# Local attention scored per 32 queries against their 160 keys, with merged scratch round trips

## What is computed

```python
h = shift_token(x)
q, k, v = split(h @ wqkv)              # 8 heads of 64
q, k = rotary_xpos(l2norm(q) * qs, l2norm(k) * ksc)
# windows of 128 queries; keys of the window before and of the own one
mask = (i < j) | (i > j + 128) | (j == -1)
attn = softmax(where(mask, -max, 8 * q @ k.T))
x = x + (attn @ v) @ wo
h = layernorm(shift_token(x)) * lg + lb
a, g = split(h @ w1 + b1)
x = x + (a * gelu(g)) @ w2 + b2
```

## Time and profile before

| | |
|---|---|
| median of 3 runs | 4971.94 us (4968.18 to 4976.64) |
| the profiled execution's own time | 4966.22 us |
| its span | 4964.4 us |
| granted clock, mean over the span | 0.959 |
| PE, DVE, ACT, POOL busy | 91%, 72%, 60%, 49% |

### The profile page before, as it was taken

The page is one execution under the profiler, slowest core; times in us unless marked ns, Lnnn a source line. Parts: engine busy times, 40 slices in busy tenths (PEclk is TensorE's granted clock), DMA queues, the critical chain, the costliest instruction groups (busy, mean ns, idle before and its releaser), DMA issues. The chain is left out here.

```text
span 4964.4 us, 269505 instructions
## 1 busy us (share of the span) xinstructions
PE 4507.8 (91%) x107928; PEld 3817.4 (77%) x107928; DVE 3564.7 (72%) x10345; ACT 2979.7 (60%) x8486; POOL 2441.6 (49%) x3196
## 2 busy tenths in 40 slices
PE   7898898678888888666999999999999999999998
PEld 6888888678888888654777777777777777777777
DVE  4666666568878887475777777777777777777775
ACT  5777777534444444354666666666666666666665
POOL 1222222267777777203555555555555555555554
PEclk8999999789999999788999999999999999999999
DMA  2343343467777777694555666555565555555554
GB/s 87 87 96 93 93 98 89 114 143 165 165 165 163 167 164 161 175 299 126 170 170 168 173 174 171 172 171 171 180 196 175 173 173 172 171 171 173 173 175 131
DMA packets 1283528, 775.96 MB, mean 156 GB/s; under 512 B 686800, under 2 KB 1179088, under 8 KB 1282256
## 3 DMA queue, kind: packets, MB, share of 16 engines
q1 hardware_dynamic: 1231888, 700.43, 53.1%
q10 hardware_dynamic: 51392, 73.02, 5.0%
HBM read 410.44 MB, written 362.68 MB: 156 GB/s over the span
## 5 line engine op out<-in xcount | busy, mean ns | idle before, releaser
L2367 ACT ACTIVATE l_prob<-l_prob,l_nb,l_rq 128x256 f32<-128x256 f32 x1024 | 601.6, 590 | 20.8 <-DVE l_nb L2193 13.1
L2033 POOL TENSOR_TENSOR l_prob<-l_prob,l_rinv 128x512 f32<-128x512 f32 x512 | 526.8, 1039 | 108.4 <-DVE l_rinv L2173 108.4
L2017 POOL TENSOR_TENSOR l_k<-l_kn,l_tab 128x512 f32<-128x512 f32 x128 | 162.5, 1270 | 614.8 <-DVE l_kn L2165 614.8
L2559 PE MATMUL lD<-l_hid,w 128*128 128x128 f32 x3072 | 364.0, 275 | 0.0
L2559 PEld LDWEIGHTS lD<-l_hid,w 128*128 128x128 f32 x3072 | 353.3, 192 | 0.0
L2551 PEld LDWEIGHTS lA<-l_hn,w 128*128 128x128 f32 x2048 | 242.9, 195 | 110.1 <-POOL l_hn L2051 61.1
L2202 DVE STREAM_TRANSPOSE l_pb<-l_prob 128x512 f32<-128x512 f32 x512 | 326.6, 676 | 0.6 <-POOL l_prob L2033 0.5
L2027 POOL TENSOR_TENSOR l_qr<-l_q 128x512 f32<-128x512 f32 x128 | 162.4, 1269 | 328.1 <-DVE l_q L2131 328.1
L1097 POOL TENSOR_TENSOR sc_aqx<-sc_late,sc_headmask 128x256 f32<-128x256 f32 x256 | 170.8, 667 | 278.9 <-PE sc_Y L1190 277.2
L1173 PE MATMUL sc_AB<-sc_aq,sc_bkx 32*32 32x32 f32 x16384 | 257.3, 198 | 37.4 <-POOL sc_bkx L1097 29.1
L497 POOL TENSOR_TENSOR rk<-rk,bkraw 128x256 f32<-128x256 f32 x64 | 54.6, 871 | 477.9 <-DVE bkraw L383 477.9
(11 more groups left out here) (276 smaller groups left out, 13707.3 us busy)
## 6 DMA issues: line engine op xcount, KB each, us to landing
scratch_pz<-l_pb SPq DMA_DIRECT2D x256, 512.0 KB, 3.0
l_pT<-scratch_pz SPq DMA_DIRECT2D x1024, 128.0 KB, 3.2
scratch_cm<-cm SPq DMA_DIRECT2D x64, 512.0 KB, 4.1
scratch_qz<-l_q SPq DMA_DIRECT2D x128, 256.0 KB, 2.9
l_qT<-scratch_qz SPq DMA_DIRECT2D x512, 64.0 KB, 2.0
scratch_kz<-l_k SPq DMA_DIRECT2D x128, 256.0 KB, 2.8
l_kT<-scratch_kz SPq DMA_DIRECT2D x512, 64.0 KB, 2.9
sc_early<-scratch_cm ACTq DMA_DIRECT2D x59, 512.0 KB, 4.7
```

Of the source, the lines that this page charges most:

```text
L2017: tt(k1[s][:], kn[s][:], wide(2, slice(0, DH)), ALU.mult)
L2033: tt(prob[s][:, pair], prob[s][:, pair], rinv[s][:, pair].unsqueeze(2).broadcast_to([P, 2, 2 * P]), ALU.mult).then_inc(Q["pn"][s].sem, 1)
L2367: last_ = nc.scalar.activation(prob[s][:, h], prob[s][:, h], ACT.Exp, scale=rq8[s][:, h:h + 1], bias=nb[s][:, h:h + 1], accum_out=sums[s][ ...
L2559: last_ = mm(bank[s][3][:, c * P:(c + 1) * P], w2[:, m, c * P:(c + 1) * P], hid[s][:, m], start=(c == 0 and m == 0), stop=(c == CC - 1 and ...
```

## The change

- **Scores.** A head pair's two matmuls (128 weight columns, 256 moving columns) become eight: for each of the four blocks of 32 queries and each head one matmul with 64 rows and 32 columns of weights, and the 160 keys that those queries can reach as moving columns.
- **Width.** `prob` is 160 wide instead of 256. Mask, maximum, exponential, normalisation and transposes work on 160 columns. The mask is one constant table `wm` with a second plane for a sequence's first window; the per-stream masks, their setup and `remask` are gone.
- **q and k.** Both are turned into one tile `qk`, written by one DMA (512 KB) and read by four (128 KB each) into the ring `qkT` of three places; in halves with w == 0 of the unit read, four more DMAs (64 KB each) put k in a second place. The write waits for both `q_turned` and `k_turned`. Before, q was read at the start of the half; now the reads stand between P's write and P's reads.
- **P.** One write of all eight heads (640 KB instead of twice 512 KB) behind the fourth `turn_p`, and eight reads of 32 to 128 KB, which all stand behind the reads of q and k. `values` waits once, at pair 0, for all eight.
- Some waits of TensorE become instructions of their own (`free_pe`), and `pT` is cleared once at the start.

```diff
                 def write_qk(s, u):
                     sp.wait_ge(S["q_turned"][s].sem, S["q_turned"][s].after(u))
+                    sp.wait_ge(S["k_turned"][s].sem, S["k_turned"][s].after(u))
...
+                    sp.dma_start(a["qkz"][s], qk[s][:].rearrange("p j y h t -> p (j y h t)")).then_inc(S["qk_out"][s].sem, 16)
+
+                def read_qk(s, u, w):
...
+                    turned = a["qkz"][s].rearrange("(i c) (j n) -> j c i n", i=BL, j=BL)
+                    cur = (2, 1)[w] * BL
                     for j in range(BL):
+                        sp.dma_start(qkT[s][32 * j:32 * j + 32, cur:cur + BL].rearrange("p i y h t -> p i (y h t)"),
+                                     turned[j]).then_inc(S["qkT"][s].sem, 16)
+                    if w == 0:
+                        for j in range(BL):
+                            sp.dma_start(qkT[s][32 * j:32 * j + 32, 0:BL, 1].rearrange("p i h t -> p i (h t)"),
+                                         turned[j][:, :, 32 * NHP:]).then_inc(S["kT"][s].sem, 16)
...
+                def write_p(s, u):
+                    sp.wait_ge(Q["p_turned"][s].sem, Q["p_turned"][s].after(u * NHP + NHP - 1))
...
+                def read_p(s, u):
...
                     for j in range(BL):
+                        for slot, lo, hi in ((0, 0, j + 1), (1, j, BL)):
+                            start = s * P * row + lo * 32 * row + (j + BL * slot - lo) * n
+                            sp.dma_start(pT[s][32 * j:32 * j + 32, lo:hi, slot].rearrange("p i h t -> p i (h t)"),
+                                         bass.AP(a["pz"].tensor, start, [[row, 32], [32 * row - n, hi - lo], [1, n]])
+                                         ).then_inc(H["pT"][s].sem, 16)
...
-                    write_p(s, u, 0)
                     if within(un):
-                        write_k(o, un)
-                    write_p(s, u, 1)
-                    read_p(s, u, 0)
+                        write_qk(o, un)
+                    write_p(s, u)
                     if within(un):
-                        read_k(o, un, wn)
-                    read_p(s, u, 1)
+                        read_qk(o, un, wn)
+                    read_p(s, u)
...
-                    for x in range(2):
-                        rows_ = slice(x * DH, (x + 1) * DH)
-                        last_ = mm(scored(s, hp, x), qT[s][rows_, :, hp], kT[s][rows_, :, :, hp].rearrange("p x i t -> p (x i) t"),
-                                   start=True, stop=True)
+                    own, back = (2, 1)[w] * BL, (1, 0)[w] * BL
+                    for i in range(BL):
+                        for x in range(2):
+                            rows_ = slice(x * DH, (x + 1) * DH)
+                            last_ = mm(scored(s, hp, x)[32 * i:32 * i + 32], qkT[s][rows_, own + i, 0, hp],
+                                       qkT[s][rows_, back + i:back + i + NR, 1, hp], start=True, stop=True)
...
-                    if hp % 2 == 0:
-                        pe.wait_ge(H[g]["pT"][s].sem, H[g]["pT"][s].after(u))
                     if hp == 0:
+                        pe.wait_ge(H["pT"][s].sem, H["pT"][s].after(u))
```

More of the change, by code:

```diff
@@ L1761, in local_stage @@
         rot, tab = two("rot", [P, 4, DH]), two("tab", [P, 4, DH])
-        wm = one("wm", [P, 2 * P])
+        wm = one("wm", [P, 2, SPAN])
         mean_w, pause, least = one("mean_w", [P, P]), one("pause", [P, NB]), one("least", [P, 1])
         x1s, dsqs = two("x1s", [P, P]), two("dsqs", [P, P])
-        mask = [two(f"mask{s}_", [P, 2, P]) for s in range(NB)]
         hT = [two(f"h{s}_", [P, CC, P + 1]) for s in range(NB)]
@@ L1789, in local_stage @@
         O = signals(nc, ctx, "oT", 2, "lg", ahead=4)
-        H = [signals(nc, ctx, "p_out:16 pT:64", 2, f"lg{g}_") for g in range(2)]
+        H = signals(nc, ctx, "p_out:16 pT:128", 2, "lh")
         I = [signals(nc, ctx, "h_in:8 rot_in:8", 2, f"li{w}_") for w in range(2)]
-        start_signals(nc, tuple(sems.values()), R, S, Z, Q, M, O, *H, *I)
+        start_signals(nc, tuple(sems.values()), R, S, Z, Q, M, O, H, *I)
         tab_made = R["tab"][0]
@@ L2259, in first @@
                     dve.wait_ge(sems["set"], 1)
-                    for s in range(NB):
-                        nc.vector.tensor_copy(mask[s][0][:, 0, :], wm[:, P:2 * P])
-                        last = nc.vector.tensor_copy(mask[s][1][:].rearrange("p x n -> p (x n)"), wm[:])
-                    last.then_inc(sems["prep"], 1)
-                    dve.wait_ge(sems["prep"], 1)
                     for s in range(NB):
@@ L2587, in half @@
                     if mlp:
-                        values(o, um, 0, layer(um, l))
-                        values(o, um, 1, layer(um, l))
+                        values(o, um, wm_, 0, layer(um, l))
+                        values(o, um, wm_, 1, layer(um, l))
                     scores(s, u, w, 0)
@@ L2594, in half @@
                     if mlp:
-                        values(o, um, 2, layer(um, l))
-                        values(o, um, 3, layer(um, l))
+                        values(o, um, wm_, 2, layer(um, l))
+                        values(o, um, wm_, 3, layer(um, l))
                     scores(s, u, w, 2)
@@ L2707, in lay_out @@
     out["eye16"] = np.ascontiguousarray(np.broadcast_to(np.eye(CH, dtype=np.float32), (P, 2, CH, CH)))
-    q, kx = np.arange(P)[:, None], np.arange(P)[None, :]
-    neg = np.float32(MASKED)
-    before, own = np.where(kx < q, neg, 0), np.where(kx > q, neg, 0)
-    out["winmask"] = np.concatenate([before, own], axis=1).astype(np.float32)
+    row, r = np.arange(P)[:, None], np.arange(160)[None, :]
+    neg, behind = np.float32(MASKED), r - row % 32
+    near = np.where((behind < 0) | (behind > P), neg, 0)
+    begin = np.where(r < P - row // 32 * 32, neg, near)
+    out["winmask"] = np.stack([near, begin], axis=1).astype(np.float32)
     n = out["x"].shape[1]
```

127 lines of the change are left out of this document (49 added, 78 removed).

## The result

The changed kernel takes 5199.26 us (median of 4 runs, 5196.34 to 5200.36) against 4970.42 before (4 runs): a ratio of 1.0457, 95% interval 1.0439 to 1.0476. It is 229 us slower.

A forecast was written before the change was run, and what follows sets the result against it. The prediction took PE's own list as the bound, with the chain through P's round trip close behind. It summed 4966 + 157 (wait) + 25 (clock) = 5148, as a median 5154 us, 3.7% slower; 8 in 10 range 4990 to 5380.

The forecast's parts named there:

- the forecast case's own range: Total time if the forecast case holds: 5060 to 5220 us, chance 0.59.
- The wait: PE at pair 0's values waits for P's last read in nearly every half, 1.3 and 3.2 us in turns.
- the predicted 7.94: Start of the mean's matmul behind the values' start, 0.9 us earlier than the 8.84 of before.
- 15.4: Issue of P's first read, us behind the values' start, in halves with four reads of q and k.
- the 2.8 taken: Seven steps from P's first read to its eighth in the issuing queue: 2.8 us, between 2.0 and 3.3.
- the wait term: Halves lengthened from 20.66 to 21.9 us by the wait for P's last read: 157 us over 127 halves.
- I allow 0.2 us per half, 25 us: Allowance for stretches at 1.2 GHz at a half's start that lengthen the chain.
- rival 2: The clock falls: 3 of 7.9 us of PE chain work at 1.2 GHz, 5250 to 5350 us; chance 0.17.
- its sign: What would show the falling clock: a granted clock under 1.00 in the steady part.
- the bounds it names: Behind the range 5060 to 5220: pace 2.1 to 3.3, landing 2.5 to 3.2, called 0.6 us either way.
- Rival 3: Narrow score tiles do not run side by side: 1.1 us more per block than before, 5550 us; chance 0.04.
- Rival 1: Quick reads, seven P steps in 2.1 and landing 2.5, leave PE the bound: about 4905 us; chance 0.15.

The follow-up runs named there:

- e1: Changed kernel with the four reads of k's second copy moved behind P's eight reads in SyncE's list; 5043.27 us, ratio 1.0144.
- e5: Changed kernel with k turned and q and k written early; SyncE's order then P's write, four q/k reads, P's reads, k's second copy; 4919.11 us.
- e6: e5 with P's second and fourth normalisations earlier on GpSimd and its first transposes ahead of the mean's subtraction on VectorE; 4838.66 us, ratio 0.9743.
- e2: Changed kernel with k turned early and the write and reads of q and k ahead of P's write in SyncE's list; 5179.01 us, ratio 1.0418.
- e8: Changed kernel with P again in two pieces of four heads, each with one write and eight reads, in the order of before; 5410.64 us, ratio 1.0891.
- e3: Changed kernel with the values' matmuls taking the identity and not waiting for P's reads, all transfers kept; wrong output; 4816.12 us, ratio 0.9685.
- e7: Changed kernel with 1 or 3 idle matmuls of 512 columns ahead of the wait for P, in both layers; 5187.38 us, ratio 1.0443.
- e9: Changed kernel with 1 or 3 idle matmuls of 512 columns ahead of the wait for P in layer 0 alone; 5169.58 us, ratio 1.0404.
- e4: Changed kernel with 4 or 12 idle matmuls of 128 columns on the identity ahead of the wait for P; 5270.50 us, ratio 1.0607.
- e10: Changed kernel with five idle matmuls of 8 columns per half of layer 0, ahead of the wait for P; 5205.08 us, ratio 1.0475.

## Why the prediction was right, and which term was off

The forecast, 5154, was 45 us under the result, which lies in the forecast case's own range.

**The wait.** Right in place and cause. PE waits for `l_pT<-scratch_pz` at the values of pair 0 in every half, 257 us in 2500. That SyncE's list is the reason is shown from both sides: e1, e5 and e6 move issues and turns of SyncE, VectorE and GpSimd alone, with the same matmuls, and the time falls by 156, 280 and 361 us; e2 leaves P's write behind the reads and keeps the loss; e8 adds issues and adds loss. Which of the merged steps is to blame for how much is not shown: no run has the narrow scores with the old round trips.

At full clock the last read does not come much later than before, and in half of the halves it comes earlier; it is wanted earlier still. Before, its data were there 22.5 behind the values' start and wanted at 23.6, by the values of pair 2. In the changed kernel, at full clock in layer 1, they are there at 15.1 + 3.2 + 2.4 = 20.7, or near 23 with eight reads of q and k, and are wanted by the values of pair 0, where PE's list ends after some 19.5 (20.66 less e3's 1.2).

**Its parts.** In layer 1, at full clock, the mean came at 7.59 for the predicted 7.94, since both score blocks together save 1.2 us and not 0.9 (e3), and P's first read at 4063.42 - 4048.35 = 15.1 for 15.4. In layer 0, without the turned output's 0.37, it stands at 3241.25 - 3226.42 = 14.8 and 3263.89 - 3246.91 = 17.0, where the prediction, less the same 0.37, has 15.0 and 17.0. P's write landed 3.7 after its issue and not some 3, but was still not waited for. Seven steps of P's reads take 3.61 - 0.43 = 3.2, for the 2.8 taken: the pace is one issue in 0.45 us whatever the size, the end that the row of before had shown and from which I moved away on the bytes. The landing is 2.4, for 2.9. These errors largely cancel: the wait term, 157 us, measures 1.05 x 127 = 133 us, if layer 1, where the branch hid it, is like e7's layer 0.

**The clock.** Here the sum was off. "I allow 0.2 us per half, 25 us" measures 0.69 (e7) and 0.73 (e9), or some 90 us over 127 halves. I had the granted clock of the earlier trace rows at 0.85 and 0.89, and took a small allowance because PE would be 90% busy. The mean clock did stay near 1, at 0.97. The prediction had named the place, a half's start, where a slow stretch lengthens the chain; what it had too small is how often one comes and how much it costs. In the timelines of 113 halves of the changed kernel (2451 to 4993 us), 58 begin behind 2.5 us or more of idle time, and 51 of these have a stretch below the full clock in their first 6 us; 51 begin behind less than 2.0 us, and none of these has. A half with such a stretch takes 22.3 us on the mean where the others take 21.0 with four reads of q and k, and 24.0 for 22.9 with eight. So rival 2's mechanism was at work, at about its lower price, beside the forecast's, and its sign, a clock under 1.00 in the steady part, was there. The Trainium skill, TensorE: Matmul & The Clock Gate, Part 1, which says that waits for transfers between bursts bring the clock down, is borne out in direction: the clock is 0.96 to 0.97 in the steady part, against 1.00 in e3, in e7's layer 0, and before. Taken for every wait, as the prediction took it, it does not hold: every half waits, and those behind a short wait stay at the full clock.

**The sum.** By layers: 22.16 - 20.42 = 1.74 us per half in layer 0's loop. In layer 1's, the branch's first and last start give (5036.6 - 3951.9)/48 = 22.60 against (4810.0 - 3806.7)/48 = 20.90, or 1.70. Over 127 halves 1.72 is 218 us; some 11 us lie outside the loops and were not followed.

That the forecast came within 45 us was in part luck: the wait was taken 24 us too long and the clock some 65 us too cheap, and the two have opposite signs. Its own range was also narrower than the bounds it names: a pace of 2.1 to 3.3 around 2.8 and a landing of 2.5 to 3.2 around 2.9 give, both at their ends, 1.1 us less or 0.8 more per half, not 0.6 either way.

**The tiles.** Rival 3 is out. From a score block in the changed kernel's timeline of PE, the first and the last of the first eight matmuls and the first of the next pass:

```profile
3227.54 0.29 PE L2482 MATMUL lB<-l_qkT 64*32 64x160 f32 x1
...
3227.59 0.32 PE L2482 MATMUL lC<-l_qkT 64*32 64x160 f32 x1
3227.67 0.29 PE L2482 MATMUL lB<-l_qkT 64*32 64x160 f32 x1
```

Eight tiles start within 0.05 us and the next pass 0.13 behind the first; the pass after it starts at 3227.86, so that the mean distance is 0.16. A pass of 160 columns by the row of 512 was 0.134, so eight tiles cost one pass and little more. The Trainium skill, TensorE: Matmul & The Clock Gate, Part 3, gives packed tiles one duration plus 4 ns for each further tile. With 0.134 for the duration that is an estimate of 0.134 + 7 x 0.004 = 0.16 for a pass: the trace agrees, though the eight starts lie 0.05/7 = 0.007 us apart and not 0.004.

**Rival 1** failed on the pace of the reads, 3.2 us for P's seven steps against its 2.1; its landing of 2.5 was near the measured 2.4. Where reads are moved away from P's path (e6), its outcome, PE as the bound, comes about.

## What to carry to other kernels

Count the DMA issues that stand ahead of the last read somebody waits for, in the issuing engine's in-order list, at 0.45 us each (here for reads of up to 128 KB, whatever their bytes), and add the wait of the reads for their own write. When pieces are merged, ask who waits first: the first user now waits for the last read of all. Put reads whose user comes late behind those whose user comes first, and never a wait for a landing ahead of an urgent write. When a busy TensorE starts to wait 1 to 3 us per round, price the clock apart from the wait: in layer 0 here it added two thirds of the wait's own cost again.

## What the runs showed that I had not expected

- **Reads at one pace.** Four reads of 128 KB take 1.77 us to issue, four of 64 KB 1.85, eight of 32 to 128 KB 3.61, and eight of half that size 3.61 too (e8).
- **A backward branch that can take 3.7 us.** 0.21 us in the loops of the kernel before and of the changed one, a median of 3.7 to 3.8 in both loops of e4 and in layer 1's of e7, with some 3 us of PE idle each time; not decided by the list's length alone (e10).
- **Order in the lists decides whether the change pays.** The narrow scores save 1.2 us of PE per half. As made the kernel has none of it, with e5's order 50 us of it, and with e6's nearly all: 130 of the 153 us that e3 gives.
